# Two adapter tables fetched already laid out by inner dimension, by loads that SyncE addresses from registers, in place of gathered rows turned on TensorE

## The reference

```python
# layer 0: w = weight[adapter_ids] (512x512 per batch), then a shared weight and a rank-16 adapter per batch
c = einsum('bsi,boi->bso', x, L0_cond_weight[itok_B_3_7])
y = einsum('bsd,od->bso', c, L0_ffn_weight) + bias
y += where(use_lora, einsum('bsr,bor->bso', einsum('bsd,brd->bsr', c, A[adapter_idx]), B[adapter_idx]), 0)
x = x + y
# layer 1: a shared weight with a rank-16 adapter per batch, then a shared weight W with 8 soft experts
h = einsum('bsi,oi->bso', x, L1_cond_weight) + bias
h += scale[id] * einsum('bsr,bor->bso', einsum('bsi,bri->bsr', x, a[id]), b[id])     # id = itok_B_1_7
H = einsum('btd,od->bto', h, W) + b
x = x + H + routed low-rank term of h (softmax over 8 experts, two global maxima)
```

## Time and profile before

| | us |
|---|---|
| median of 3 runs | 124.84 (124.45 to 125.58) |
| the profiled execution | 123.69 |
| its span | 122.0 |
| PE busy | 117.1 (96%) |
| DVE busy | 82.7 (68%) |
| ACT busy | 56.0 (46%) |
| POOL busy | 22.5 (18%) |
| DMA, mean | 170 GB/s, 20.79 MB |

### The profile page before, as it was taken

How to read it: one execution, slowest core, us unless ns; L and a number is a source line. 1 busy time by engine, 2 the same in 40 slices (tenths; PEclk the granted TensorE clock), 3 DMA queues, 4 the chain that set the end, 5 groups by cost and what they waited for, 6 DMA issues and landing times.

```text
span 122.0 us, 1916 instructions
## 1 busy us (share of the span) xinstructions
PE 117.1 (96%) x703; PEld 100.6 (82%) x703; DVE 82.7 (68%) x170; ACT 56.0 (46%) x93; POOL 22.5 (18%) x30
## 2 busy tenths in 40 slices
PE   6999999999989999999999999999999999999990
PEld 2488878887879897898989999999989787688890
DVE  0589898966788979677987623687965376504831
ACT  4279498539969685759195313212520110230000
POOL 3067884060514615000002000000000000000000
PEclk9999999999999999999999999999999999999999
DMA  3999999979965999999277000000000000000972
GB/s 97 393 417 310 356 376 316 355 237 329 313 238 149 269 277 301 256 282 251 56 238 296 0 0 0 5 0 0 0 0 5 0 0 0 0 0 0 343 257 96
DMA packets 7865, 20.79 MB, mean 170 GB/s; under 512 B 1200, under 2 KB 1584, under 8 KB 7856
## 3 DMA queue, kind: packets, MB, share of 16 engines
q1 hardware_dynamic: 4944, 10.87, 26.9%
q0 software_dynamic: 2624, 9.44, 24.5%
q10 hardware_dynamic: 288, 0.36, 0.9%
HBM read 16.39 MB, written 2.10 MB: 152 GB/s over the span
## 4 chain that ended last, share of the span: by engine, by line
PE 90%; ACT 4%; DVE 2%; issue 1%; ACTq 0%; DVEq 0%
PE bank L850 70%; PE bank L953 3%; PE bank L963 3%; PE bank L959 3%; PE bank L956 3%; PE bank L887 2%; PE bank L1033 1%; ACT a L416 1%; DVE w_lo L686 1%; ACT c_row L424 1%; ACT w_hi L388 1%; PE bank L944 1%; PE bank L1102 1%; PE bank L1096 1%; DVE low L556 1%
## 5 line engine op out<-in xcount | busy, mean ns | idle before, releaser
L539 DVE TENSOR_TENSOR w_lo<-w_in,w_hi 128x1024 fp32r<-128x1024 f32 x16 | 19.3, 1224 | 4.4 <-ACT w_hi L382 4.3
L337 POOL DMA_INDIRECT w_in<-in_W,rows_i x16 | 17.1, 1069 | 25.5 <-DVE w_lo L539 14.2
L382 ACT CAST w_hi<-w_in 128x1024 fp32r<-128x1024 f32 x16 | 16.2, 1052 | 5.1 <-DMA w_in<-in_W,rows_i 5.1
L850 PE MATMUL bank<-c_hi,w_hi 128*128 128x256 f32 x64 | 18.2, 284 | 0.0
L850 PE MATMUL bank<-c_lo,w_hi 128*128 128x256 f32 x64 | 18.1, 283 | 0.0
L850 PE MATMUL bank<-c_hi,w_lo 128*128 128x256 f32 x64 | 18.1, 283 | 0.0
L850 PE MATMUL bank<-m_hi,x_hi 128*128 128x512 f32 (+1 forms) x36 | 13.9, 385 | 0.0
L850 PE MATMUL bank<-w_hi,x_hi 128*128 128x512 f32 x32 | 13.3, 416 | 0.0
L850 PE MATMUL bank<-m_hi,x_lo 128*128 128x512 f32 (+1 forms) x36 | 13.2, 368 | 0.0
L850 PE MATMUL bank<-m_lo,x_hi 128*128 128x512 f32 (+1 forms) x36 | 13.2, 367 | 0.0
L850 PE MATMUL bank<-w_hi,x_lo 128*128 128x512 f32 x32 | 12.6, 393 | 0.0
(11 more groups left out here) (177 smaller groups left out, 237.7 us busy)
## 6 DMA issues: line engine op xcount, KB each, us to landing
w_in<-in_W SPq DMA_DIRECT2D x5, 512.0 KB, 6.1
x_in<-in_x SPq DMA_DIRECT2D x4, 512.0 KB, 7.6
out_dram<-w_in SPq DMA_DIRECT2D x7, 256.0 KB, 2.8
be<-late_t SPq DMA_DIRECT2D x16, 69.0 KB, 6.6
b<-low_t SPq DMA_DIRECT2D x16, 64.0 KB, 4.9
w_in<-in_W SPq DMA_DIRECT2D x1, 1024.0 KB, 6.1
late_t<-in_late SPq DMA_DIRECT2D x1, 552.0 KB, 3.6
w_in<-in_W ACTq DMA_DIRECT2D x1, 256.0 KB, 3.6
```

Of the source, the lines that this page charges most:

```text
L337: nc.gpsimd.indirect_dma_start(w_in[:, slot, half * h:half * (h + 1)], None, W0, row).then_inc(w_landed[b][h], 16)
L382: nc.scalar.copy(part(w_hi[:, b % 2], h), raw(b, h)).then_inc(w_hi_done, 1)
L539: nc.vector.tensor_tensor(part(w_lo[:, b % 2], h), raw(b, h), f32(part(w_hi[:, b % 2], h)), ALU.subtract).then_inc(w_lo_done, 1)
L850: ins = mm(o, st, mv, start=start and n == 0, stop=stop and n == len(parts) - 1)
```

## The change

The tables `g0` and `g1` are split. `g0` keeps only factor B of layer 0 (2 KB a row) and is still gathered by POOL. Two new tables in device memory hold the rest already transposed for each adapter: `f0` (A of layer 0, per adapter 128 partitions x 64 numbers) and `f1` (A and B of layer 1, per adapter 128 x 2 x 64). POOL's DMA of `g1` is gone. SP reads, for each of the 8 batches, one row number from `adapter_i` into a register and issues one DMA whose source address comes from it: 8 for `f1`, then W1, then 8 for `f0`, each of pieces of 256 bytes (64 KB and 32 KB a DMA). The three sets of four transposes are gone; the casts and subtractions that followed them remain and read the landed tile in SBUF, taking every fourth number, and `adapters_high` is four instructions of 384 columns instead of one of 1536. On PE the product that needs b1 stands after `layer_a(1)`. `load_x(2)` and `load_x(3)` wait for `a0_done` and `a1_done`, the end of the subtraction, where they waited for the transposes.

```diff
-        rows1 = x_in[:, NP - 1].rearrange("p c s -> p (c s)")
-        rows0 = x_in[:, NP - 2].rearrange("p c s -> p (c s)")
+        turned1 = x_in[:, NP - 1].rearrange("p c s -> p (c s)").rearrange("p (t n) -> p t n", t=2)
+        turned0 = x_in[:, NP - 2, 0:2].rearrange("p c s -> p (c s)")
+        rows0 = x_in[:, NP - 2, 2:4].rearrange("p c s -> p (c s)")
...
         def pairs(ap):
-            return ap.rearrange("p (n k) -> p n k", k=K2)
+            return ap.rearrange("p (i k c) -> p c i k", c=C, k=K2)
+
+        def by_chunk(ap):
+            return ap.rearrange("p (k c) -> p c k", c=C)
...
+            def load_w1():
+                slot, half = w_slot("w1"), C * D // 2
+                sp.wait_ge(w_hi_done, 2)
+                sp.wait_ge(w_lo_done, 2)
+                for h in range(2):
+                    sp.dma_start(w_in[:, slot, half * h:half * (h + 1)],
+                                 W1[:, half * h:half * (h + 1)]).then_inc(w1_landed[h], 16)
...
+            sp.wait_ge(adapters_done, 2)
+            for b in range(NB):
+                first = sp.value_load(adapter_i[RANK * b:RANK * b + 1, 1:2], min_val=0, max_val=(NL1 - 1) * RANK)
+                t = f1[bass.ds(first, RANK)].rearrange("r q n -> (r q) n").rearrange("p (t n) -> p t n", t=2)
+                sp.dma_start(turned1[:, :, RANK * C * b:RANK * C * (b + 1)], t).then_inc(f1_landed, 16)
+            load_w1()
+            for b in range(NB):
+                first = sp.value_load(adapter_i[RANK * b:RANK * b + 1, 0:1], min_val=0, max_val=NL0 * RANK)
+                t = f0[bass.ds(first, RANK)].rearrange("r q n -> (r q) n")
+                sp.dma_start(turned0[:, RANK * C * b:RANK * C * (b + 1)], t).then_inc(f0_landed, 16)
...
             spread(b0, b0_parts, 0, b0_landed[0])
-            sp.wait_ge(a0_ready, 1)
+            sp.wait_ge(a0_done, 1)
             load_x(2)
...
             spread(b0, b0_parts, 1, b0_landed[1])
-            sp.wait_ge(a1_ready, 1)
+            sp.wait_ge(a1_done, 1)
             load_x(3)
...
-            nc.gpsimd.indirect_dma_start(rows1, None, g1, row1).then_inc(g1_landed, 16)
...
-            def adapters_high(t, ps):
-                return nc.scalar.copy(t[:, :, 1:], pairs(ps).unsqueeze(2).to_broadcast([P, C * NP, G - 1, K2]))
+            def adapters_high(t, turned):
+                for c in range(C):
+                    last = nc.scalar.copy(t[:, c, :, 1:], pairs(turned)[:, c].unsqueeze(2).to_broadcast([P, NP, G - 1, K2]))
+                return last
...
-            act.wait_ge(b1_ready, 1)
-            nc.scalar.copy(flat(b1_hi), bank[7][:]).then_inc(b1_hi_done, 1)
...
             save_c0(0)
+            act.wait_ge(f1_landed, 16 * NB)
+            nc.scalar.copy(b1_hi, by_chunk(turned1[:, 1])).then_inc(b1_hi_done, 1)
             w_high(2)
+            save_c0(1)
             act.wait_ge(be_ready, 1)
             act.wait_ge(s_landed, 16)
             nc.scalar.activation(be_parts[:, 0, 0:D], bank[4][:], ACT.Copy, scale=s_c[:]).then_inc(be_hi_done, 1)
-            save_c0(1)
             c0_high(0)
-            act.wait_ge(a0_ready, 1)
-            adapters_high(a0, bank[6][:]).then_inc(a0_hi_done, 1)
+            act.wait_ge(f0_landed, 16 * NB)
+            adapters_high(a0, turned0).then_inc(a0_hi_done, 1)
...
-            pe.wait_ge(g1_landed, 16)
+            layer_a(0)
             pe.wait_ge(ident_done, 1)
-            turn_rows(bank[7], rows1[:, D:2 * D]).then_inc(b1_ready, 1)
-            layer_a(0)
```

More of the change, by code:

```diff
@@ L53, in place, with build @@
         at += w
-def build(nc, x, W0, W1, W23, g0, g1, scale, early, late, out):
+def build(nc, x, W0, W1, W23, g0, f0, f1, scale, early, late, out):
     ctx = ExitStack()
@@ L676, in _ @@
             nc.vector.tensor_tensor(ae_f[:], aet[:, :, NS:], ae_f[:], ALU.add).then_inc(ae_summed, 1)
+            dve.wait_ge(b1_hi_done, 1)
+            nc.vector.tensor_tensor(b1_lo, by_chunk(turned1[:, 1]), f32(b1_hi), ALU.subtract).then_inc(b1_lo_done, 1)
             w_low(2)
@@ L682, in _ @@
             dve.wait_ge(a0_hi_done, 1)
-            nc.vector.tensor_tensor(a0[:, :, 0], pairs(bank[6][:]), f32(a0[:, :, 1]), ALU.subtract).then_inc(a0_done, 1)
+            nc.vector.tensor_tensor(a0[:, :, :, 0], pairs(turned0), f32(a0[:, :, :, 1]), ALU.subtract).then_inc(a0_done, 1)
             for h in range(2):
@@ L703, in _ @@
             dve.wait_ge(a1_hi_done, 1)
-            nc.vector.tensor_tensor(a1[:, :, 0], pairs(bank[5][:]), f32(a1[:, :, 1]), ALU.subtract).then_inc(a1_done, 1)
+            nc.vector.tensor_tensor(a1[:, :, :, 0], pairs(turned1[:, 0]), f32(a1[:, :, :, 1]), ALU.subtract).then_inc(a1_done, 1)
             x1_sum(0, 0)
@@ L914, in layer_b @@
                     pe.wait_ge(be_done, 1)
-                else:
-                    pe.wait_ge(a1_hi_done, 1)
-                    pe.wait_ge(a1_done, 1)
                 if h == 0:
@@ L939, in layer_low1 @@
                 low_rank(bank[7][:, 0:2 * S], a1, i, x_hi[:, i], x_lo[:, i]).then_inc(low1_ready, 1)
-            def turn_rows(o, rows):
-                for c in range(C):
-                    to = chunk(o[:], c)
-                    last = nc.tensor.transpose(to, chunk(rows, c),
-                                               ident[:])
-                return last
             def m_chunk(c):
@@ L974, in _ @@
             product(bank[5][0:2 * NS, :], parts).then_inc(ae_ready, 1)
-            pe.wait_ge(g1_landed, 16)
+            layer_a(0)
             pe.wait_ge(ident_done, 1)
-            turn_rows(bank[7], rows1[:, D:2 * D]).then_inc(b1_ready, 1)
-            layer_a(0)
+            pe.wait_ge(ae_saved, 1)
+            pe.wait_ge(m_lo_done, 3)
+            for c in range(C):
+                last = nc.tensor.transpose(bank[2][:, 2 * NS * c:2 * NS * (c + 1)], chunk(ae_rows, c),
+                                           ident[0:2 * NS, 0:2 * NS])
+            last.then_inc(aet_ready, 1)
+            layer_a(1)
             pe.wait_ge(b1_hi_done, 1)
@@ L985, in _ @@
             product(bank[4][:], parts).then_inc(be_ready, 1)
-            pe.wait_ge(ae_saved, 1)
-            pe.wait_ge(m_lo_done, 3)
-            for c in range(C):
-                last = nc.tensor.transpose(bank[2][:, 2 * NS * c:2 * NS * (c + 1)], chunk(ae_rows, c),
-                                           ident[0:2 * NS, 0:2 * NS])
-            last.then_inc(aet_ready, 1)
-            pe.wait_ge(g0_landed, 16)
-            turn_rows(bank[6], rows0[:, 0:D]).then_inc(a0_ready, 1)
-            layer_a(1)
             turn_c0(0)
```

44 lines of the change are left out of this document (20 added, 24 removed).

## The result

The changed kernel takes **131.75 us** (median of four runs, 130.88 to 132.9) against 124.91 us for the kernel before on the same chip (four runs, 124.45 to 125.58): ratio 1.059, 95% interval 1.053 to 1.066. It is slower. The profiled execution took 131.03 us for a span of 129.3; before it was 123.69 and 122.0, so +7.3 us are to be explained.

A forecast was written before the change was run, and what follows sets the result against it. PE's restart, behind ACT's cast of a0, decides: f0 complete at 33.0, casts 1.62 and 2.86 more give 37.5 us against 34.14, +3.4. Median 124.84 + 3.4 = 128.2 us, range 124.1 to 134.

The forecast's parts named there:

- The step on SP: SP's load, register arithmetic and DMA issue per batch: 1.23 us, of which 0.48 issue and 0.75 register work.
- f0 complete: Landing of the last f0 DMA on SP's queue: at 33.0 us, where a0's cast began at 29.94.
- f1: Landing of SP's f1 DMAs: by 22.3 to 24.5 us, late for b1 but costed at nothing.
- The transposes at nothing: Three sets of four transposes off PE, 1.32 us: worth nothing as long as ACT's list decides the restart.
- `load_x(2)` and `load_x(3)` at nothing: Loads of x now waiting for the subtractions: just in time or up to about 1 us late, taken as covered.
- The direction, slower with 0.62: Whole kernel: slower by more than about 1%, chance 0.62; within 1% 0.28, faster 0.10.
- the slow read: Rival: reading every fourth number costs twice per column, adding 1.2 us to a0's casts; chance 0.15.
- the stretch behind the restart: After 34.14 us PE is busy but for 0.3 us; the change takes nothing out of that part.
- Four casts of 384 columns, 0.41 each, +0.3.: ACT's cast of a0 in four instructions: 1.62 us instead of 1.34, at 0.81 ns a column.
- PE's clock falls in the gap: Rival: PE's 4 to 5 us pause lowers its clock, +2.0 us, 130.2; chance 0.3 among the slow cases.
- The copies of b0: Copies behind f0 on SP's queue: landed at about 35.5 us, before the restart at 37.5, costed at nothing.
- f0 lands in time, no change: Rival: cheap register work, step about 0.8 us, restart moves -0.9 to +0.3 us, likeliest 124.4; chance 0.25.

The follow-up runs named there:

- e12: The kernel before with its twelve transposes left out, gathered rows read as they lie, over twelve runs: 124.84 us, ratio 1.002.
- e3: The changed kernel with source addresses fixed in the program and tables stored with ranks as neighbours: 125.22 us over ten runs, ratio 0.999.
- e1: The changed kernel with tables stored so 16 numbers lie next to each other instead of reading every fourth: 129.31 us, ratio 1.045.
- e8: The kernel before, all gathers and transposes kept, plus SP's sixteen register-addressed steps copying f1 and f0 into spare output rows: 130.06 us, ratio 1.050.
- e2: The changed kernel with the sixteen source addresses fixed in the program, no register work on SP, every fourth number still read: 129.01 us, no ratio.
- e9: The changed kernel with neighbouring ranks, plus 16 idle matmuls on PE in the gap before the first product on a0: 129.92 us, ratio 1.048.
- e4: The changed kernel plus 20 idle matmuls on PE in the gap before the first product on a0: 131.67 us.
- e10: Half of the change against the kernel before: f1 by SP's register-addressed loads with neighbours, layer 0's A still gathered and turned: 123.93 us, ratio 0.997.

## Why the prediction was right and wrong

**Right, with the numbers as forecast.** PE's restart carries 5.3 of the 7.3 us, and a0's cast is a link of that path. The step on SP: 1.23 us forecast, 1.40 and 1.20 measured. The split was less good: 0.48 for the issue and 0.75 for register work were set; for f0 it is 0.34 and 0.86, of which the load is 0.27. The Trainium skill, "DMA: Bandwidth & Descriptors", "Latency and other measured facts", has about 600 ns as the floor of one such load; here the medians are 0.274 and 0.280 us, and four of the sixteen took 0.46, 0.46, 0.48 and 0.71, so the measurement decides against that floor for a load from SBUF on SP. The forecast's sum didn't rest on it. f0 complete: 33.0 forecast, 33.3 measured. f1: 22.3 to 24.5 forecast, 24.1 measured. The transposes at nothing: shown by e12, and by e3's ratio. `load_x(2)` and `load_x(3)` at nothing: behind the restart PE waits once for 0.3 us, as before, and once for 0.2, and for no x. The direction, slower with 0.62, is the one that came.

**Wrong, the size**: +3.4 us forecast, +7.3 measured between the profiled executions, +6.8 between the medians (131.75, inside the range of 124.1 to 134). Two terms failed, both named as rivals and both left out of the sum: the slow read makes +1.7 us to the restart, and the stretch behind the restart, which the forecast left as it was, is +2.0.

*"Four casts of 384 columns, 0.41 each, +0.3."* This is the step that failed first. They take 0.79 us each, 3.08 from the first to w1's cast where 1.62 was forecast: +1.46. The subtraction of a0, by the same reads 1.09 us instead of 0.69, came out from behind w1's cast: +0.26. f0 itself came 0.34 later than forecast, DVE's two next rows were 0.12 shorter together: 37.48 + 1.46 + 0.26 + 0.34 - 0.12 = 39.42. e1 took this term away alone and found 37.35. The reason given for costing the read once, a constant time per column, was taken from reads of neighbours and carried to a read that no row showed; the rule on the other side was at hand. The Trainium skill, "SBUF — State Buffer", "Door 1: The DMA port swizzle", lets each access to a new 16-byte line pay, and a stride of four f32 is a new line each time. The same passage names four fp32 as how far one can stride for free; at a stride of exactly four the runs show a price. The traces agree with the rule on new lines in direction, and give the price that the page lacks, though no run shows that the line is the reason: 0.79 against 0.44 us for 384 columns on ACT, 1.09 against 0.62 for 512 (the cast of b1, after and e1), and 1.09 against 0.69 on DVE. A chance of 0.15 was too low.

*"PE's clock falls in the gap", a rival with a chance of 0.3.* It fell, and the sum had no term for it. Its price as a rival was set at +2.0. The stretch behind the restart is +2.0 longer, but the clock makes 1.5 of it up to the next transposes of c0, and 1.0 to 1.3 net by single executions; a1's slow casts are likely most of the rest. The two agree by luck in part: the price was read off the first nine matmuls of the trace, 0.45 us each, where the granted clock of the earlier trace rows stands in the top digit. The slow casts made the gap longer, 5.3 us against 3.2 in e1, but the clock fell in e1 too: the late data alone was enough for it.

**Right by luck.** The copies of b0 were costed at nothing "before 37.5". e8 shows 5.2 us behind that word, of wait and clock. It did no harm to the forecast only because a0 was as late; but the rival "f0 lands in time, no change" leaned on the same cover, and with cheap registers and f0 at 29.4 us, as in e2, the copies are issued at 24.1 and in time: there the rival was sound. In between, with f0 just in time and SP's list as long as in e8, b0 takes over.

## What to carry to other kernels

Work that leaves an engine is worth what that engine's next wait lets through; read which list releases it before counting the work removed. Moving fetches to another queue moves everything behind them: list each DMA that stands behind the new ones, with its date of need, and don't let one late item serve as the cover of another. A layout read by every fourth f32 cost nearly twice on ACT here and over half as much again on DVE, so a table that is laid out by the host anyway should be laid out for neighbours.

## What the runs showed of the hardware

- A register load from SBUF on SP: 0.27 us in the median, up to 0.71; the whole register-addressed step 1.20 to 1.40 us against 0.70 us and a little more without the register work (e2).
- The issue of a DMA on SP differs with its form: with the address from a register 0.34 us for 128 x 64 numbers and 0.54 us for 128 x 2 x 64; with fixed addresses 0.46 and 0.67 us for the same pieces (e2, medians); 0.53 us for 128 x 64 numbers into device memory (e8).
- Small DMAs of 32 KB behind W1's 1 MB landed 5.9 us after the last issue in e2, 3.6 in the changed kernel, where that issue came 10 us after W1's.
- TensorE's granted clock fell to the lower level in or behind gaps of 5.3, 4.0 (e8), 3.2 (e1), 3.1 (e2) and 2.8 us (e9), and in e12's profiled execution behind 2.2 and 1.1 us that lie 5 us apart: there the 34 matmuls behind the restart took 5.84 us against 4.57. It stayed up behind 1.9 and 2.2 us that lie 14 us apart (e4), 1.45 and 0.7 (e10), 1.6 (e3) and 0.7 (before).
- From such a restart to the next transposes of c0 the same matmuls took 4.41 us (before, e4) and 4.51 us (e9) at the upper level, and 5.78 (e1), 5.94 (the changed kernel) and 6.81 us (e2) where the clock had fallen.
